# Gathered rows without columns of ones: the softmax weights copied into the weighed rows by ScalarE

## The chip, the core and the metric

The kernel runs on one core of a Trainium2 chip. The metric is the device time of one execution in microseconds (us). A core has a matrix engine (TensorE, PE in the profile; PEld is its weight load), a vector engine (VectorE, DVE), a scalar engine (ScalarE, ACT), GpSimd (POOL), which also issues the indirect DMAs, and SyncE (SP), which only issues DMAs and handles semaphores. Each engine runs its own instructions in order; between engines only semaphores order the work.

## The reference

Two graph layers over the same graph with 12500 nodes of 256 features (8 heads of 32) and 200000 edges that are sorted by their destination. Layer 0 is a transformer layer, layer 1 a graph attention layer. The part that the change touches is the softmax over the edges of a node, in both layers:

```
layer 0: score = sum(K[src] * Q[dst]) / sqrt(32) + edge_bias        (per head)
layer 1: score = leaky_relu(el[src] + er[dst], 0.2)                 (per head)
ex   = exp(score - segment_max(score, dst)[dst])
out  = segment_sum(ex / segment_sum(ex, dst)[dst] * value[src], dst)
```

`value` is V in layer 0 and `feat` in layer 1. The kernel divides last: it sums `ex * value` and `ex` itself per node and divides the one by the other.

## The kernel before

**Phases.** In order of time: a short start that works out which tile of 128 nodes each step serves; the projection of all nodes (98 tiles), which stores the tables `kv_tab` (K and V) and `q_tab`; the edge phase of layer 0; the dense phase between the layers (98 tiles: projection, norms, feed-forward part, and the table `ft_tab` of layer 1); the edge phase of layer 1; a final pass of 98 tiles.

**The edge phase.** It has 880 steps, in 110 blocks of 8 (`ST`). A step takes one span of 256 edges (two chunks of 128) and one tile of 128 nodes. There are 782 spans; where a span reaches into the next tile, it is used by a second step. POOL gathers the rows of a span with two indirect DMAs of 128 rows each (`gathers`, line 525) into a ring of 18 spans in layer 0 and 32 in layer 1. Before it reuses a place of the ring it waits until the last weighing of that place is done (`ev_made`, line 520).

**A step on the engines**, at these distances in steps (in `turn` of each engine's `edge_phase`):
- ACT makes the one-hot matrices of the edges' nodes (`distances`, `onehots`), some steps ahead.
- PE (`spread`) multiplies them with the queries (layer 0) or with `er` (layer 1), two steps ahead.
- DVE makes the scores: `product` and `reduce` in layer 0, `el_er` in layer 1 (with `members`, line 1227, which makes the transposed one-hots).
- Once per block, the maxima are found by scans on DVE with transposes on PE in between (`chunk_scans`, `row_scans`, `whole_scans`, `below_maximum`), and at s == 3 ACT makes the exponentials of the block before (`weights`, line 688, tile `ex`).
- 12 steps after the scores, DVE multiplies the gathered values with `ex` (`weigh`, line 1284, tile `ev`, which has places for 4 steps), and PE (`agg`) multiplies the one-hots with `ev` and so sums over the edges. Two steps later DVE adds the result to the running sums (`add`, line 1299); ACT stores four steps' sums at a time (`sum_store`).

**The columns of ones.** A value row is kept as 8 heads of 33 floats, of which the 33rd is 1.0. So `weigh` leaves `ex` itself in the 33rd column, and `agg` sums it with the values: this gives the denominator. The ones are written once into the four `kvo` buffers (line 1067) and into `fo` (line 1357), and then stored with every tile's rows in `kv_tab` (520 floats a row: 256 of K, 264 of V) and `ft_tab` (272 floats: 264 of `feat`, 8 of `el`). Every gather brings them back.

**Order of the queues.** SP starts the load of a step's queries or nodes (lines 375, 444) and tells DVE that a span has landed (`landed`, line 387), which POOL has signalled (line 532). At the head of each block DVE, SP and POOL load 8 or 16 registers from tables (`slots`, `spans_of`), which tell where each step's rows lie.

Of the kernel before, what the change touches and what calls it, by code (L numbers as in the profile page):

```python
# [26 lines left out]
P = 128  # L27
# [15 lines left out]
KVW = D + HV  # L43
FTW = HV + H
# [91 lines left out]
def build(nc, x, last, edges, span_src, Wq, Wk, Wv, Wp, bp, g1, b1n, g2, b2n, W1, b1, W2, b2,  # L136
          Wl, bl, Wg, al, ar, gb, out):
    ctx = ExitStack()
    with ctx:
# [150 lines left out]
        for name in """arep_made pat ats_made ohd oh_made oht_tr  # L290
            oht_cp oh0_made qexp prodd redd sadd smade s_tr scan_a rows_mm rows_cp row carried xy_cp cols_mm scan_b rx_made
            r_exp r_mm rm_made m_tr dmade ex_made ev_made agg accd resc init0 init1""".split():
            E_[name] = sem(name)
# [27 lines left out]
        def hv(ap):  # L321
            return ap.rearrange("p (h w) -> p h w", h=H)
# [257 lines left out]
        def _(act):  # L580
# [105 lines left out]
            def weights(B):  # L686
                act.wait_ge(E_["dmade"], B.c + 1)
                act.activation(ex[:, B.par, :], df[:, :], ACT.Exp).then_inc(E_["ex_made"], 1)  # L688

            def sum_store(layer, B, h):  # L690

                act.wait_ge(E_["accd"], B.c * ST + 4 * h + 4)
                r = (2 * B.n + h) * 4 * P
                act.dma_start(sums[r:r + 4 * P, :].rearrange("(p j) w -> p j w", j=4),
                              acc[:, B.par, 4 * h:4 * h + 4, :]).then_inc(acs[layer][B.par], 16)
# [7 lines left out]
            def edge_phase(layer):  # L703
                def turn(B):
                    A = B.on(-1)
                    for s in range(ST):
# [33 lines left out]
                        if s == 3 and A.live:  # L740
                            weights(A)

# [71 lines left out]
        def _(pe):  # L814
# [84 lines left out]
            def agg(B, s):  # L899
                pe.wait_ge(E_["ev_made"], B.c * ST + s + 1)  # L900
                o = sums_bank(B, s)
                mm(o, oh[:, B.tri, 2 * s, :], ev[:, s % 4, 0, :], True, False)
                mm(o, oh[:, B.tri, 2 * s + 1, :], ev[:, s % 4, 1, :], False, True).then_inc(E_["agg"], 1)
# [148 lines left out]
        def _(dve):  # L1052
# [13 lines left out]
            for kvo in kvos:  # L1066
                c0.did(V.memset(kvo[:, D:KVW], 1.0))
# [30 lines left out]
            def q_turn(t, slots, laps):  # L1098
# [15 lines left out]
                if not isinstance(t, int) or t >= 2:  # L1114
                    dve.wait_ge(S_["q_mm"], t - 1)
                    c = slots[2]
                    wait(dve, S_[f"q_st{c}"], 48 * laps[2])
                    V.tensor_copy(hv(kvos[c][:, D:KVW])[:, :, 0:HD],
                                  hv(bank[4 + c % 2][:, 0:D])).then_inc(S_["q_vq"], 1)
# [92 lines left out]
            def el_er(B, s, at):  # L1212
                dve.wait_ge(S_["rows_rdy"], B.c * ST + s + 1)
                dve.wait_ge(E_["qexp"], B.c * ST + s + 1)
                V.tensor_tensor(hc(sred[:, :])[:, :, 2 * s:2 * s + 2], step_rows(1, at)[:, :, HV:FTW].rearrange("p c h -> p h c"),  # L1215
                                bank[2 + s % 2][:, 0:2 * H].rearrange("p (c h) -> p h c", h=H),
                                ALU.add).then_inc(E_["sadd"], 1)
# [62 lines left out]
            def weigh(layer, B, s, at):  # L1280
                if s == 0:
                    dve.wait_ge(E_["ex_made"], B.c + 1)
                val = step_rows(0, at)[:, :, KVW - HV:KVW] if layer == 0 else step_rows(1, at)[:, :, 0:HV]
                V.tensor_tensor(ev[:, s % 4, :, :].rearrange("p k (h w) -> p k h w", h=H),  # L1284
                                val.rearrange("p k (h w) -> p k h w", h=H),
                                hc(ex[:, B.par, :])[:, :, 2 * s:2 * s + 2].rearrange("p h k -> p k h")
                                .unsqueeze(3).to_broadcast([P, 2, H, HD + 1]),
# [69 lines left out]
            c1.seq(V.memset(fo[:, 0:HV], 1.0))  # L1357
# [26 lines left out]
            def m_turn(t):  # L1384
# [20 lines left out]
                if on(4, t):  # L1405
                    dve.wait_ge(S_["m_mm2"], t - 3)
                    wait(dve, S_["m_sft"], 16 * (t - 4))
                    V.tensor_tensor(hv(fo[:, 0:HV])[:, :, 0:HD], hv(bank[7][:, 0:D]), hv(v_lge[:, 0:D]),
                                    ALU.add).then_inc(S_["m_fo"], 1)
                    V.tensor_tensor(fo[:, HV:FTW], bank[7][:, D:D + H], v_lge[:, D:D + H],  # L1410
# [96 lines left out]
```

## Time and profile before

| | |
|---|---|
| median of 3 runs | 6099.34 us (6095.61 to 6106.41) |
| the profiled execution | 6105.02 us, of which the span of the trace is 6103.1 us |
| busy share of the span | PE 89%, PEld 71%, DVE 81%, ACT 52%, POOL 61% |
| mean granted clock of TensorE | 0.902 of full speed |
| DMA | 1313.62 MB, mean 215 GB/s |
| edge phase, layer 0 | products from 377.8 to 2772.1 us |
| edge phase, layer 1 | gathers from 3767.8 to 5843.4 us |

A busy share is a mean over phases with different limits, so each phase is read by itself. A row of the windows view gives the busy time of each engine in a stretch and the number of its instructions; a row of the groups view gives the count of a kind of instruction, its total and mean time, and how long its engine had been idle before it and what ended that. Instructions of an engine overlap a little: the mean length of one is longer than the time from its start to the next one's start.

### The profile page before, as it was taken

The numbers are of one execution on the slowest core, as the hardware profiler recorded it, in microseconds if no ns is written. First come the engines' busy times: TensorE is split into PE (matmuls) and PEld (weight loads), VectorE is DVE, ScalarE is ACT, GpSimd is POOL, SyncE is SP. The second block draws the span as 40 slices with busy tenths as digits, with TensorE's granted clock in tenths as the row PEclk, the third lists the DMA queues.
The fourth block names the chain that finished last, engine by engine and source line by source line (L and its number), as shares of the span: only waits on it lengthen the run. The fifth ranks groups of instructions, "written<-read, shape, count | busy, mean of one in ns | idle before, by whom it ended". The sixth has DMA issues, their size and how long they took to land. (4 is left out here: it accounts for less than half of the span.)

```text
span 6103.1 us, 127510 instructions
## 1 busy us (share of the span) xinstructions
PE 5456.4 (89%) x26094; PEld 4304.6 (71%) x26094; DVE 4918.7 (81%) x12464; ACT 3153.0 (52%) x10275; POOL 3719.7 (61%) x4022
## 2 busy tenths in 40 slices
PE   8978888888888888887999998899999999999988
PEld 5556666666666666666999997677777777777766
DVE  4479999999999999996777775778778778777764
ACT  3455555555555555552333334555555556555533
POOL 1146666666666666662444445777777777777733
PEclk9999999999999999998999998777777777777789
DMA  5678888888888888883222223777777777777767
GB/s 177 211 225 282 275 271 274 271 271 273 272 273 270 271 273 273 272 269 108 85 84 84 84 84 110 213 222 218 217 219 221 219 219 222 216 217 219 221 194 230
DMA packets 723027, 1313.62 MB, mean 215 GB/s; under 512 B 109087, under 2 KB 502131, under 8 KB 722420
## 3 DMA queue, kind: packets, MB, share of 16 engines
q0 software_dynamic: 200192, 634.41, 37.2%
q1 hardware_dynamic: 444802, 422.18, 23.3%
q10 hardware_dynamic: 77426, 250.73, 10.6%
q14 instruction: 445, 3.65, 0.2%
q8 instruction: 162, 2.65, 0.2%
HBM read 964.16 MB, written 342.73 MB: 214 GB/s over the span
## 5 line engine op out<-in xcount | busy, mean ns | idle before, releaser
L816 PE MATMUL bank<-ev,oh 128*128 128x264 f32 x7040 | 2287.7, 455 | 90.7 <-DVE ev L1284 89.6
L525 POOL DMA_INDIRECT Gf<-kv_tab,srcs x1564 | 1541.1, 985 | 858.9 <-issue 465.4
L525 POOL DMA_INDIRECT Gf<-ft_tab,srcs x1564 | 1600.3, 1023 | 483.2 <-issue 420.1
L816 PEld LDWEIGHTS bank<-ev,oh 128*128 128x128 f32 x7040 | 1465.4, 221 | 346.8 <-DVE ev L1284 126.1
L816 PE MATMUL bank<-Gf 128*128 128x128 f32 (+3 forms) x6480 | 1261.7, 346 | 21.3 <-ACT Gf L805 14.4
L816 PE MATMUL bank<-qs,oht 128*128 128x256 f32 x3520 | 955.7, 394 | 319.9 <-DVE prod L1193 319.8
L1284 DVE TENSOR_TENSOR ev<-Gf,ex 128x528 f32<-128x528 f32 x1760 | 1236.8, 703 | 2.1 <-ACT ex L688 1.3
L816 PEld LDWEIGHTS bank<-Gf 128*128 128x128 f32 x6480 | 965.7, 191 | 220.2 <-issue 98.1
L621 ACT ACTIVATE absd<-lane,dlocs 128x128 f32<-128x128 f32 x3520 | 1112.8, 389 | 4.2 <-DVE bms L1166 3.7
L816 PEld LDWEIGHTS bank<-qs,oht 128*128 128x128 f32 x3520 | 599.6, 190 | 543.8 <-issue 370.9
L1299 DVE SCALAR_TENSOR_TENSOR acc<-acc,same,bank 128x264 f32<-128x264 f32 x1540 | 738.3, 479 | 28.3 <-PE bank L816 25.4
L1193 DVE TENSOR_TENSOR prod<-Gf,bank 128x512 f32<-128x512 f32 x880 | 600.5, 682 | 116.8 <-SPq L387 106.4
L502 POOL TENSOR_TENSOR vr<-vr,mhalf 128x1 f32<-128x1 f32 x392 | 248.5, 634 | 717.5 <-DVE vr L1373 418.8
L626 ACT ACTIVATE oh<-absd,ones 128x512 f32<-128x512 f32 x880 | 631.6, 718 | 10.9
L1199 DVE TENSOR_REDUCE sred<-prod 128x16 f32<-128x512 f32 x880 | 596.2, 678 | 0.3
L582 ACT ACTIVATE oht<-bank 128x512 f32<-128x512 f32 x440 | 261.2, 594 | 299.2 <-PE bank L819 293.7
L816 PEld LDWEIGHTS bank<-erq,prod 128*128 128x128 f32 x1760 | 352.5, 271 | 65.8 <-issue 34.8
L770 ACT ACTIVATE Gf<-bank,Gf 128x128 f32<-128x128 f32 x784 | 223.6, 369 | 289.4 <-PE bank L816 289.4
L816 PE MATMUL bank<-erq,prod 128*128 128x8 f32 x1760 | 345.1, 306 | 18.7 <-DVE sred L1215 18.0
L1215 DVE TENSOR_TENSOR sred<-Gf,bank 128x16 f32<-128x16 f32 x880 | 147.3, 167 | 246.9 <-PE bank L816 120.3
L652 ACT ACTIVATE rm<-bank,oh 128x8 f32<-128x8 f32 x220 | 78.6, 357 | 512.3 <-PE bank L816 506.3
L816 PEld LDWEIGHTS bank<-erq,oht 128*128 128x128 f32 x1760 | 274.5, 217 | 84.6 <-issue 53.5
(160 smaller groups left out, 6095.4 us busy)
## 6 DMA issues: line engine op xcount, KB each, us to landing
sums<-acc ACTq DMA_DIRECT2D x440, 528.0 KB
qs<-q_tab SPq DMA_DIRECT2D x880, 128.0 KB
qs<-dst_tab SPq DMA_DIRECT2D x880, 128.0 KB
Gf<-sums SPq DMA_DIRECT2D x196, 132.0 KB, 2.1
kv_tab<-Gf SPq DMA_DIRECT2D x98, 260.0 KB, 2.1
Gf<-in_x SPq DMA_DIRECT2D x196, 128.0 KB, 2.1
Gf<-kv_tab,srcs POOLq DMA_INDIRECT x1564
Gf<-ft_tab,srcs POOLq DMA_INDIRECT x1564
```

Source lines behind the costliest of these rows:

```text
L502: pool.tensor_tensor(vr[:, 2 * k + 1:2 * k + 2], vr[:, 2 * k:2 * k + 1], mhalf[:, :], ALU.pow).then_inc(done, 1)
L525: pool.indirect_dma_start(out=rows[layer][:, m % SLOTS[layer], k, :], out_offset=None, in_=tab, in_offset=bass.IndirectOffsetOnAxis(ap=src ...
L582: act.activation(o, i_, ACT.Copy).then_inc(s, 1)
L621: act.activation(absd[:, g % 2, k, :], lane[:, :], ACT.Abs, scale=-1.0, bias=dloc[:, B.n, 4 * g + k:4 * g + k + 1]).then_inc(E_["ohd"], 1)
L626: act.activation(oh[:, B.tri, 4 * g:4 * g + 4, :].rearrange("p c n -> p (c n)"), absd[:, g % 2, :, :].rearrange("p c n -> p (c n)"), ACT.R ...
L770: act.activation(gT[:, f * P:(f + 1) * P], bank[2 + f // 4][:, (f % 4) * P:(f % 4 + 1) * P], ACT.Gelu, bias=v_b1[:, f:f + 1]).then_inc(S_[ ...
L816: return nc.tensor.matmul(o, a, r, start=first, stop=end)
L1193: V.tensor_tensor(prod[:, s % 2, :, :], step_rows(0, at)[:, :, 0:D], bank[2 + s % 2][:, :].rearrange("p (k n) -> p k n", k=2), ALU.mult).t ...
L1199: V.tensor_reduce(hc(sred[:, :])[:, :, 2 * s:2 * s + 2].rearrange("p h c -> p c h"), prod[:, s % 2, :, :].rearrange("p k (h w) -> p k h w" ...
L1215: V.tensor_tensor(hc(sred[:, :])[:, :, 2 * s:2 * s + 2], step_rows(1, at)[:, :, HV:FTW].rearrange("p c h -> p h c"), bank[2 + s % 2][:, 0: ...
L1284: V.tensor_tensor(ev[:, s % 4, :, :].rearrange("p k (h w) -> p k h w", h=H), val.rearrange("p k (h w) -> p k h w", h=H), hc(ex[:, B.par, : ...
L1299: V.scalar_tensor_tensor(acc[:, B.par, s, :], prev, same[:, B.n * ST + s:B.n * ST + s + 1], sums_bank(B, s), ALU.mult, ALU.add).then_inc(E ...
```

## The change

The 33rd columns leave the tables. `kv_tab` has 512 floats a row, `ft_tab` 264. `weigh` multiplies 32 floats a head instead of 33 and leaves the 33rd column of `ev` alone. A new function on ACT, `weights_column`, copies the 16 values of `ex` (2 chunks of 8 heads) of a step into the 33rd columns, one step ahead of PE's `agg` in the order of the queues (`step_at(B, s - 11)` against `s - 12`). Before it writes, ACT waits until `agg` of four steps earlier has read that place of `ev`. `agg` waits for the new semaphore `exs_made` in addition to `ev_made`. The writing of ones (lines 1067 and 1357) is gone.

```
-KVW = D + HV
-FTW = HV + H
+KVW = 2 * D
+FTW = D + H
...
+            def weights_column(B, s):
+
+                if s == 0:
+                    act.wait_ge(E_["ex_made"], B.c + 1)
+                p, r = step_at(B, s - 4)
+                if p.live:
+                    act.wait_ge(E_["agg"], p.c * ST + r + 1)
+                copy(ev[:, s % 4, :, :].rearrange("p k (h w) -> p k h w", h=H)[:, :, :, HD],
+                     hc(ex[:, B.par, :])[:, :, 2 * s:2 * s + 2].rearrange("p h k -> p k h"), E_["exs_made"])
...
                         if s == 3 and A.live:
                             weights(A)
+                        C, r = step_at(B, s - 11)
+                        if C.live:
+                            weights_column(C, r)
...
             def agg(B, s):
+                pe.wait_ge(E_["exs_made"], B.c * ST + s + 1)
                 pe.wait_ge(E_["ev_made"], B.c * ST + s + 1)
...
-            for kvo in kvos:
-                c0.did(V.memset(kvo[:, D:KVW], 1.0))
...
-                    V.tensor_copy(hv(kvos[c][:, D:KVW])[:, :, 0:HD],
-                                  hv(bank[4 + c % 2][:, 0:D])).then_inc(S_["q_vq"], 1)
+                    V.tensor_copy(kvos[c][:, D:KVW], bank[4 + c % 2][:, 0:D]).then_inc(S_["q_vq"], 1)
...
-                V.tensor_tensor(hc(sred[:, :])[:, :, 2 * s:2 * s + 2], step_rows(1, at)[:, :, HV:FTW].rearrange("p c h -> p h c"),
+                V.tensor_tensor(hc(sred[:, :])[:, :, 2 * s:2 * s + 2], step_rows(1, at)[:, :, D:FTW].rearrange("p c h -> p h c"),
...
-                val = step_rows(0, at)[:, :, KVW - HV:KVW] if layer == 0 else step_rows(1, at)[:, :, 0:HV]
-                V.tensor_tensor(ev[:, s % 4, :, :].rearrange("p k (h w) -> p k h w", h=H),
+                val = step_rows(0, at)[:, :, D:KVW] if layer == 0 else step_rows(1, at)[:, :, 0:D]
+                V.tensor_tensor(ev[:, s % 4, :, :].rearrange("p k (h w) -> p k h w", h=H)[:, :, :, 0:HD],
                                 val.rearrange("p k (h w) -> p k h w", h=H),
                                 hc(ex[:, B.par, :])[:, :, 2 * s:2 * s + 2].rearrange("p h k -> p k h")
-                                .unsqueeze(3).to_broadcast([P, 2, H, HD + 1]),
+                                .unsqueeze(3).to_broadcast([P, 2, H, HD]),
                                 ALU.mult).then_inc(E_["ev_made"], 1)
...
-            c1.seq(V.memset(fo[:, 0:HV], 1.0))
...
-                    V.tensor_tensor(hv(fo[:, 0:HV])[:, :, 0:HD], hv(bank[7][:, 0:D]), hv(v_lge[:, 0:D]),
-                                    ALU.add).then_inc(S_["m_fo"], 1)
-                    V.tensor_tensor(fo[:, HV:FTW], bank[7][:, D:D + H], v_lge[:, D:D + H],
+                    V.tensor_tensor(fo[:, 0:D], bank[7][:, 0:D], v_lge[:, 0:D], ALU.add).then_inc(S_["m_fo"], 1)
+                    V.tensor_tensor(fo[:, D:FTW], bank[7][:, D:D + H], v_lge[:, D:D + H],
```

## Rows read from the trace of the kernel before

**Rows 1.** Windows: from:to, length, busy us (count) per engine, PE clock, DMA share, GB/s

```profile
100.00:200.00 100.00, 96.60 (x321) 53.64 (x322) 49.17 (x161) 41.49 (x130) 17.52 (x32) 1.00 0.63 211
...
600.00:2500.00 1900.00, 1618.35 (x7827) 1246.08 (x7826) 1813.01 (x3651) 1095.57 (x3217) 1212.23 (x1237) 1.00 0.87 272
3000.00:3600.00 600.00, 600.00 (x3936) 551.50 (x3935) 430.27 (x1397) 210.39 (x697) 291.32 (x444) 1.00 0.27 85
4000.00:5800.00 1800.00, 1675.44 (x7038) 1326.07 (x7037) 1433.56 (x4089) 1059.58 (x3895) 1387.08 (x1356) 0.74 0.78 219
```

**Rows 2.** Groups by form, 600 to 2500 us (layer 0): busy us, mean ns | idle before, releasers

```profile
L525 POOL DMA_INDIRECT Gf<-kv_tab,srcs x1237 | 1213.1, 981 | 687.8 <-issue 350.7 <-DVE ev L1284 274.4 <-DMA Gf<-kv_tab,srcs 62.7
...
L1284 DVE TENSOR_TENSOR ev<-Gf,ex 128x528 f32<-128x528 f32 x696 | 490.4, 705 | 0.0
L1193 DVE TENSOR_TENSOR prod<-Gf,bank 128x512 f32<-128x512 f32 x695 | 474.2, 682 | 80.6 <-SPq L387 74.9 <-issue 5.7
...
L1299 DVE SCALAR_TENSOR_TENSOR acc<-acc,same,bank 128x264 f32<-128x264 f32 x608 | 292.4, 481 | 0.3 <-PE bank L816 0.3
...
L1269 DVE TENSOR_TENSOR df<-S,bank 128x128 f32<-128x128 f32 x86 | 24.1, 281 | 0.0
```

**Rows 3.** Timeline of DVE at the head of a block of layer 0

```profile
1615.99 0.28 DVE L1208 TENSOR_TENSOR S<-sred,bms 128x128 f32<-128x128 f32 x1
1617.16 0.69 DVE L1193 TENSOR_TENSOR prod<-Gf,bank 128x512 f32<-128x512 f32 x1 [0.89 <-SPq L387]
```

**Rows 4.** Waits of SP's queue, 600 to 2500 us: total us, times, longest

```profile
SPq L375 <- PE bank L816: 717.2, 442, 2.5
SPq L387 <- POOLq L532: 1.1, 2, 0.7
```

**Rows 5.** Groups by form, 0 to 30 us (the start)

```profile
L1082 DVE TENSOR_TENSOR same<-tile_of 128x879 f32<-128x879 f32 x1 | 1.1, 1074 | 0.0
```

**Rows 6.** Groups by form, 4000 to 5800 us (layer 1)

```profile
L525 POOL DMA_INDIRECT Gf<-ft_tab,srcs x1356 | 1387.9, 1024 | 413.2 <-issue 357.5 <-DMA Gf<-ft_tab,srcs 35.3 <-DVE ev L1284 20.4
...
L582 ACT ACTIVATE erq<-er_all 128x8 f32 x760 | 151.3, 199 | 91.5 <-issue 74.4 <-PE bank L816 16.6
```

**Rows 7.** Line 525, the gathers of layer 1: shortest/median/longest ns, first and last start

```profile
L525 POOL DMA_INDIRECT Gf<-ft_tab,srcs x1564: 942/947/1753, 3767.8 to 5843.4; - x196
```

**Rows 8.** Timeline in layer 1: start us, length us, idle before it

```profile
5820.65 0.70 DVE L1284 TENSOR_TENSOR ev<-Gf,ex 128x528 f32<-128x528 f32 x1
5820.71 1.45 POOL L525 DMA_INDIRECT Gf<-ft_tab,srcs  x1 [0.30 <-issue]
...
5822.47 0.95 POOL L525 DMA_INDIRECT Gf<-ft_tab,srcs  x1 [0.30 <-issue]
```

**Rows 9.** Timeline in layer 1: ACT and PE around a step's weighed sum

```profile
4610.56 0.28 ACT L663 ACTIVATE ats<-bank 128x128 f32<-128x128 f32 x1 [3.13 <-PE bank L819]
...
4611.10 1.26 ACT L621 ACTIVATE absd<-lane,dlocs 128x128 f32<-128x128 f32 x4
...
4612.27 0.20 ACT L582 ACTIVATE erq<-er_all 128x8 f32 x1
...
4612.89 0.91 PE L816 MATMUL bank<-ev,oh 128*128 128x264 f32 x3
```

**Rows 10.** Timeline at the start and at the head of the dense phase

```profile
3.02 1.12 DVE L1067 MEMSET Gf<- 128x264 f32 x4
4.06 0.11 DVE L1068 TENSOR_SCALAR last_t<-last_i 128x7 int32<-128x7 int32 x1
...
10.22 3.27 PE L816 MATMUL bank<-oh,ones 128*128 128x440 f32 x4 [10.22 <-DVE ev L1074]
...
2816.09 0.28 DVE L1357 MEMSET Gf<- 128x264 f32 x1 [22.48 <-DMA Gf<-in_L_gnn_b_lin]
2816.45 0.17 DVE L1389 TENSOR_SCALAR Gf<-Gf 128x8 f32<-128x8 f32 x1
```

**Rows 11.** DMA queue of the gathers, 1000 to 1500 us: packets, MB, share of 16 engines

```profile
q0 software_dynamic: 26055, 86.73, 59.5%
```

More of the change, by code:

```diff
@@ L291, in build @@
             oht_cp oh0_made qexp prodd redd sadd smade s_tr scan_a rows_mm rows_cp row carried xy_cp cols_mm scan_b rx_made
-            r_exp r_mm rm_made m_tr dmade ex_made ev_made agg accd resc init0 init1""".split():
+            r_exp r_mm rm_made m_tr dmade ex_made exs_made ev_made agg accd resc init0 init1""".split():
             E_[name] = sem(name)
```

## Prediction

> **What bounds the kernel now.** I read the windows first, because the limit changes with the phase [rows 1]. In the first stretch (projection) PE is busy for 96.6 of 100 us, in the dense phase for 600 of 600: these two are PE's, and the change takes no matrix work away. In layer 0's edge phase DVE is busy for 1813 of 1900 us and PE for only 1618. In layer 1's, DVE has 20% left and PE 7%, and POOL is busy for 1387 of 1800 us, which looks loose and is not.
>
> In layer 0 the groups tell where DVE's missing 87 us are [rows 2]: 80.6 of them stand ahead of the product, 0.3 ahead of the sum, none ahead of the weighing. The 1900 us hold 695 products, which is 87 blocks, and 87 times 0.89 us [rows 3] is 77 us: one gap at each block's head. SP's signal is named as its releaser. But SP waits for landed rows only 2 times in this stretch, and 442 times for PE [rows 4], so the rows are there early; DVE's own 16 register loads at a block's head are the simpler cause. POOL is ahead too: 274 us of its idle time are waits for a free place in the ring. So layer 0 goes at the rate at which DVE gets through its list, 1900/695 = 2.73 us a step.
>
> In layer 1 POOL's group [rows 6] adds up to the window: 1387.9 us busy and 413.2 idle, and the idle time is 0.305 us ahead of each of 1356 DMAs. That is no waiting: 0.30 also stands before DMAs that waited for nothing [rows 8]. POOL issues without a break, at 1.024 + 0.305 = 1.329 us each. All 1564 take 2078 us, and the gathers last from 3767.8 to 5843.4 [rows 7]. Layer 1 goes at POOL's issue rate.
>
> **Weigh, in layer 0.** It loses 16 of 528 elements. Two DVE products of two tensors of other lengths give the price of an element: 879 take 1074 ns [rows 5], 128 take 281 ns [rows 2], so (1074 - 281)/751 = 1.056 ns, and 16 cost 16.9 ns. The product with 512 elements, 682 ns against 705, agrees within 6 ns, though it reads PSUM. Nothing else on DVE changes in a step, and DVE hardly waits, so 880 x 16.9 ns = **14.9 us** fall out. Bounds: 0 (the output now leaves gaps, and a gapped write could cost what it saves) and 880 x 23 ns = 20 us.
>
> **Weigh, in layer 1.** DVE has room here, so directly its saving is worth nothing. But half of the gathers take 947 ns or less, and the mean is 1024 [rows 7, 6]. A case shows why [rows 8]: the DMA at 5820.71, issued while a weighing was running, took 1.45 us, the next one 0.95. Its extra 0.50 us end at 5821.21, when the weighing (from 5820.65) has streamed its 528 elements, 528 x 1.056 = 0.56 us. So a gather that is issued into a weighing waits for the end of its streaming. As a check: steps are 1800/761 = 2.365 us, the chance to hit one is 0.56/2.365 = 24%, the mean wait 0.28 us, together 66 ns for a DMA, of 77 measured. With 512 elements each such wait ends 16.9 ns earlier: 1564 x 0.24 x 16.9 ns = **6.3 us**, on the path. Bounds: 0, if the phases shift so that hits become more frequent, and 1564 x 16.9 = 26 us, if every gather waited; I take the middle price because it explains the mean.
>
> The Trainium skill (SBUF — State Buffer, section "Who interferes with whom") says that a VectorE operation with two SBUF inputs contends with GpSimd instructions that read SBUF, but infers that such an operation does not hold up the generation of descriptors. By the first half the 6.3 us stand, by the second they would be 0 and the time 6.3 us longer. The case above speaks for the first.
>
> **The column copies on ACT.** The nearest row is a copy of 128x8 from SBUF in 199 ns [rows 6]; 16 elements need hardly more, and four distances of 128x128 take 1.26 us together [rows 9], 0.32 us each, so neighbours overlap. I take 0.2 us: 1760 x 0.2 = 352 us of ACT time. It lies beside other work: ACT is busy for 58% and 59% of the edge phases [rows 1] and would go to 65% and 67%. What matters is whether a column is later than the weighed rows that PE needs anyway. The tightest place I found is in layer 1 after the link sums [rows 9]: ACT comes out of a 3.13 us wait at 4610.56, has its four distances done at 4612.36 and the copy of `er` at 4612.47; the column would be ready at about 4612.7, and PE took up the weighed sum at 4612.89. It fits by 0.2 us. ACT's other operations behind the column move back by 0.2 us each step and are caught up in ACT's next wait for PE, which is 3.13 us here. The added wait for `agg` of four steps earlier is long fulfilled in ACT's order. PE's added wait instruction has no row; from 0 to some 50 ns a step it stays inside PE's slack (layer 1: 1675.44/761 = 2.20 us busy of 2.365, so 0.16 us). Cost 0; if this cover is gone it costs as in the third rival.
>
> **Start and head of the dense phase.** The four memsets delay the next DVE instruction from 3.02 to 4.06 us, and PE's first product waits for that chain [rows 10]: **1.0 us** (at least 0, if something behind hides it). The memset at 2816.09 delays its successor by 0.36 us at a point where all wait for DVE: **0.4 us**.
>
> **Bytes.** Gathered rows are 1.5% (layer 0) and 3% (layer 1) shorter; the gathers take 59.5% of the DMA engines' time [rows 11] and nobody waits for them. Stores of the tables in the two PE-bound phases shrink likewise. 0 us.
>
> **Sum.** 14.9 + 6.3 + 1.0 + 0.4 = 22.6 us. The profiled execution took 6105.0 us (1.9 beyond its span), which gives 6082.4. It stands 5.7 us above the median of 6099.3, so against the median the forecast is **6076.7 us**, -0.37%. A measurement of this kernel can tell about 0.2%, 12 us, from no change.
>
> **Rivals.**
> 1. *The block's head takes layer 0's saving back.* If the gap [rows 3] is a wait for SP at a pace that does not depend on DVE, a shorter weighing only lengthens it. For it: SP is named. Against it: SP's own waits. Only 7.7 us remain: 6091.6. Chance 0.12.
> 2. *The weighing gets no shorter*, since its output now has gaps. Against it: the elements are single floats in either case. 1.4 us remain, 6097.9. Chance 0.07.
> 3. *Slower: the columns come late in layer 1.* ACT reaches the column only behind its long groups, PE then idles before the weighed sum. It decides from a mean lateness of 0.16 us a step, where PE's busy 2.20 us plus waiting pass POOL's 2.365. At 0.3 us a step the phase grows by 880 x 0.14 = 120 us, less the 16 us of layer 0 and the start: 6203. For it: a margin of only 0.2 us at one step in eight. Against it: ACT idles about 3 us twice a block. Chance 0.06.
> 4. *Slower: the gathers of layer 0 slow down.* Rows of exactly 2048 bytes start at equal places modulo 2048. DMA engines are busy for 0.87 [rows 1], so if the gathers' 59.5% took 22% longer they would be full; at 40% longer the phase grows by 0.87 + 0.24 = 1.11, 11% of 2394 us, to 6350. No row speaks for it. The Trainium skill (DMA: Bandwidth & Descriptors, "Latency and other measured facts") reports loss at row pitches of large powers of two, from 512 KiB up, which is far from here. Chance 0.02.
> 5. *More than forecast*: layer 1's gathers are hit much less, as they fall elsewhere between the weighings, up to 26 us there: 6057. Chance 0.06.
>
> The forecast itself has the remaining 0.67, with its own range 6069 to 6086. Taking in rival 1 and the nearer half of rival 5, the range is 6067 to 6094. Faster by over 0.2% (below 6087.1): the forecast and rival 5, less a little for noise, 0.69. Within: rivals 1 and 2 and that noise, 0.22. Slower: rivals 3 and 4 and what I have not seen, 0.09.
>
> **What would show it.** Right: weighings of 128x512 at 686 to 688 ns, DVE's gap at a block's head still 0.89 us, layer 0's products taking 2379 us from first to last instead of 2394; in layer 1 POOL's mean at 1020 ns and its last gather about 2069 us after its first; new ACT copies near 0.2 us, with no idle time of PE ahead of the weighed sum that ends on ACT. Wrong: a gap at the block's head that grows by 0.14 us (rival 1), weighings at 703 ns (rival 2), PE idle in front of `agg` with ACT's copy as its releaser (rival 3), POOL's mean unchanged or higher.

## The result, and the profile after

| | before | after |
|---|---|---|
| median (5 runs each) | 6099.43 us (6095.61 to 6106.41) | 6133.27 us (6126.67 to 6146.65) |
| ratio, 95% interval | | 1.0051 (1.004 to 1.0063) |
| the profiled execution, its span | 6105.02, 6103.1 us | 6129.33, 6127.4 us |
| layer 0, first product to last weighing | 2413.3 us | 2398.3 us |
| between, to the first gather of layer 1 | 976.6 us | 977.6 us |
| layer 1, first gather to last sum | 2107.9 us | 2146.6 us |
| start, last pass | 377.8, 227.4 us | 377.7, 227.2 us |

The forecast was 6076.7 us, faster; the kernel became slower by 0.5%. Layer 0 gave what was forecast, layer 1 took 38.7 us more.

Windows of the changed kernel (columns as in [rows 1]):

```profile
600.00:2500.00 1900.00, 1625.68 (x7876) 1250.67 (x7874) 1812.34 (x3671) 1174.73 (x3937) 1215.61 (x1246) 1.00 0.84 271
4000.00:5800.00 1800.00, 1643.72 (x6879) 1303.56 (x6879) 1387.08 (x3997) 1122.88 (x4557) 1390.43 (x1345) 0.74 0.75 213
```

In layer 0 DVE does more in the same time at the same busy share. In layer 1 every engine but ScalarE does less (PE 6879 instructions instead of 7038), and only ScalarE, which has the copies, is clearly busier (POOL by 3 us): PE idles for 156 us of the 1800 instead of 125. DVE's groups in layer 0, 600 to 2500 us:

```profile
L1295 DVE TENSOR_TENSOR ev<-Gf,ex 128x512 f32<-128x512 f32 x700 | 480.7, 687 | 0.0
L1204 DVE TENSOR_TENSOR prod<-Gf,bank 128x512 f32<-128x512 f32 x699 | 476.1, 681 | 80.5 <-SPq L387 74.1 <-issue 6.3
```

687 ns a weighing against 705, and the idle time at the blocks' heads unchanged (80.5 against 80.6 us) [rows 2]. The groups of layer 1, 4000 to 5800 us, PE's first, then its weight load, ScalarE's copies, POOL's gathers:

```profile
L829 PE MATMUL bank<-ev,oh 128*128 128x264 f32 x2973 | 1146.7, 522 | 110.4 <-DVE ev L1295 56.8 <-ACT ev L582 52.1 <-issue 0.2
...
L829 PEld LDWEIGHTS bank<-ev,oh 128*128 128x128 f32 x2974 | 675.1, 251 | 229.6 <-ACT ev L582 70.0 <-issue 62.8
...
L582 ACT ACTIVATE ev<-ex 128x16 f32<-128x16 f32 x744 | 162.4, 218 | 3.1
...
L525 POOL DMA_INDIRECT Gf<-ft_tab,srcs x1345 | 1391.4, 1035 | 409.9 <-issue 352.9 <-DMA Gf<-ft_tab,srcs 34.4 <-DVE ev L1295 22.6
```

The same group of the kernel before has 72.5 us of idle time of PE ahead of the weighed sum, 71.7 of them ended by DVE:

```profile
L816 PE MATMUL bank<-ev,oh 128*128 128x264 f32 x3044 | 1182.2, 525 | 72.5 <-DVE ev L1284 71.7 <-issue 0.2
```

Now it is 110.4, and a new releaser, ScalarE's copy, stands beside DVE. This is what the forecast had named as the sign of its third rival. One place of it (timeline of the changed kernel, start, length, idle time before):

```profile
4560.51 1.26 ACT L621 ACTIVATE absd<-lane,dlocs 128x128 f32<-128x128 f32 x4
...
4561.68 0.19 ACT L582 ACTIVATE erq<-er_all 128x8 f32 x1
4561.78 0.21 ACT L582 ACTIVATE ev<-ex 128x16 f32<-128x16 f32 x1
4561.90 0.70 ACT L626 ACTIVATE oh<-absd,ones 128x512 f32<-128x512 f32 x1
4562.04 0.74 PEld L829 LDWEIGHTS bank<-ev,oh 128*128 128x128 f32 x4 [0.52 <-ACT ev L582]
4562.05 0.94 PE L829 MATMUL bank<-ev,oh 128*128 128x264 f32 x3 [0.43 <-ACT ev L582]
```

It is the fourth step of a block, the very place of [rows 9]: the column follows the four distances and `er`, ends at 4561.99, and PE has been idle for 0.43 us. But the sums per step of a block, worked out from the records of PE over the 110 blocks, show that this is only a part. Mean idle time of PE ahead of the weighed sum in layer 1, steps 0 to 7, and the shortest distance from the end of a weighing to the start of its sum:

```
step      0     1     2     3     4     5     6     7    shortest distance
before   0.01  0.01  0.01  0.00  0.05  0.15  0.19  0.37   0.05 us
after    0.01  0.05  0.00  0.27  0.05  0.17  0.19  0.45   0.15 us
```

Steps 3 and 1 have late columns. At step 7 no column is late (it ends 1.1 us ahead at least), and yet PE waits longer, and no sum starts less than 0.15 us behind its weighing, where it was 0.05. So there were two suspects.

That PE, and no longer POOL, sets the pace can be read at the end of the layer. Before, PE's last weighed sum ends 31.8 us after the last gather starts; in the changed kernel it ends 57.9 us after it. POOL still issues without a break (1391.4 + 409.9 us fill the window), and PE falls behind it, as the ring of 32 spans allows. The last gather itself starts 2088.2 us after the first, 12.6 us later than before; the part on why the prediction was wrong comes back to this.

### The profile page after: what moved, and what is told of

Its sections match the earlier page's. It is cut to its first block and busy times, and to the rows that moved or that the text cites. A ratio compares the mean times of both kernels' runs of the same rounds, so it can differ in the third digit from the quotient of the medians.

```text
span 6127.4 us, 131243 instructions
## 1 busy us (share of the span) xinstructions
PE 5453.4 (89%) x26094; PEld 4304.3 (70%) x26094; DVE 4886.3 (80%) x12459; ACT 3347.9 (55%) x12035; POOL 3722.2 (61%) x4022
## 5 line engine op out<-in xcount | busy, mean ns | idle before, releaser
L525 POOL DMA_INDIRECT Gf<-ft_tab,srcs x1564 | 1612.9, 1031 | 483.2 <-issue 416.4
L1295 DVE TENSOR_TENSOR ev<-Gf,ex 128x512 f32<-128x512 f32 x1760 | 1205.0, 685 | 2.5 <-ACT ex L688 1.6
L582 ACT ACTIVATE ev<-ex 128x16 f32<-128x16 f32 x1760 | 385.2, 219 | 16.7 <-DVE acc L1310 5.0
```

Of the source, the lines that this page charges most:

```text
L525: pool.indirect_dma_start(out=rows[layer][:, m % SLOTS[layer], k, :], out_offset=None, in_=tab, in_offset=bass.IndirectOffsetOnAxis(ap=src ...
L582: act.activation(o, i_, ACT.Copy).then_inc(s, 1)
```

## The experiments

The theories, by the letters that the expectations use: **L**, late columns; **W**, the second wait of the weighed sum costs 0.10 us by itself; **A**, ScalarE's load alone; **C**, nothing of layer 1 but the clock or heat that layer 0 leaves. Later W is split: **W1**, any second wait costs it; **W2**, only if the wait that PE really waits for stands in the separate instruction. **P** is the prediction's claim on gathers: one that is issued into a weighing waits for the end of its streaming. Kernels under one heading ran on one chip beside the kernel before (under "Where the wait has its price" two chips); ratios are to it, with 95% intervals.

### First four: a chip of 7316 us, on which small waits do not show

Layer 0 changed alone (tables and weighing of layer 1 as before, its sum with one wait):

```
-FTW = D + H
+FTW = HV + H
...
-                        if C.live:
+                        if C.live and layer == 0:
...
-                pe.wait_ge(E_["exs_made"], B.c * ST + s + 1)
+                if B.layer == 0:
+                    pe.wait_ge(E_["exs_made"], B.c * ST + s + 1)
                 pe.wait_ge(E_["ev_made"], B.c * ST + s + 1)
...
```

> The change in layer 0 only; layer 1 keeps its columns of ones, its 528-element weighing and its single wait. If the loss is all in layer 1 (every theory below), layer 0 keeps its 15 us and layer 1 its 2108 us: 6084 to 6086 us, ratio 0.9975. If shorter weighings in layer 0 shift something that layer 1 or the dense phase gives back, it stays near 6099.

The kernel before with one wait more:

```
             def agg(B, s):
+                pe.wait_ge(E_["ex_made"], B.c + 1)
                 pe.wait_ge(E_["ev_made"], B.c * ST + s + 1)
```

> The kernel before, but the weighed sum on TensorE waits for a second semaphore (ex_made), which has long been reached; nothing else changes. Theory W (a second wait in front of the weighed sum costs 0.10 us wherever the sum would start as soon as the weighing ends): in layer 1 the shortest distance from the end of a weighing to the sum rises from 0.05 to 0.15 us, at three or four steps of a block, so 0.3 to 0.4 us a block and 15 to 40 us in all: 6115 to 6140. Theory L (late columns alone cost the time): a second wait is free, 6099.

The kernel before with the copies, into a tile that nobody reads (ScalarE waits for its own earlier copies instead of for PE's sums):

```
...
+                wait(act, E_["exs_made"], B.c * ST + s - 3)
+                copy(spare[:, :, :].rearrange("p k (h w) -> p k h w", h=H)[:, :, :, HD - s % 4],
+                     hc(ex[:, B.par, :])[:, :, 2 * s:2 * s + 2].rearrange("p h k -> p k h"), E_["exs_made"])
...
```

> The kernel before, with ScalarE's 1760 small copies at the same places, into a spare tile that nobody reads and nobody waits for (the copies wait for ScalarE's own earlier copies instead of for TensorE's sums). If ScalarE's added load is what costs (its other results reach TensorE later): layer 1 loses 20 us or more, 6120. Theories L and W both say that the load is covered: 6095 to 6105.

The changed kernel with the columns one step earlier:

```
                         if s == 3 and A.live:
                             weights(A)
-                        C, r = step_at(B, s - 11)
-                        if C.live:
+                            weights_column(A, 0)
+                        C, r = step_at(B, s - 10)
+                        if C.live and r:
                             weights_column(C, r)
```

> The changed kernel with every column one step earlier in ScalarE's order (step 0's right behind the exponentials, then step s - 10 instead of s - 11). The sum still has two waits. Theory L: no sum finds its column missing, 0.3 us a block is back in layer 1, about 35 us: 6095 to 6100. Theory W: half of the loss stays, 0.10 us wherever the sum meets the end of a weighing: 6105 to 6120.

Measured: this chip ran the kernel before in 7316.19 us, 20% above the 6099 of all I had reasoned from. Ratios 1.0059 (1.0036 to 1.0082), 1.0006 (0.9989 to 1.0022), 0.9998 (0.9983 to 1.0014), 0.9996 (0.9981 to 1.0011). The window of layer 1 in the run with the second wait shows the other regime:

```profile
5000.00:6800.00 1800.00, 1473.20 (x5372) 1146.67 (x5373) 1106.63 (x3118) 813.11 (x2981) 1067.52 (x1032) 0.65 0.62 167
```

No engine is near full, PE neither: 1800 us hold 1032 gathers instead of 1356, and the clock is 0.65. A tenth of a microsecond lost or won at PE's sum does not show in the end there. The distances can still be read: shortest 0.05 us with one wait (first and third), 0.15 us with two (second and fourth).

The first run missed its expectation of 0.9975: it was slower than the kernel before. Its layer 0 took 2988 us, the other three 2924 to 2934. Its trace shows late columns at work in layer 0. PE's groups there, 1000 to 2500 us, first of this run, then of the run with the early columns:

```profile
L829 PE MATMUL bank<-ev,oh 128*128 128x264 f32 x1784 | 522.3, 419 | 193.2 <-ACT ev L582 187.9 <-issue 5.4
```

```profile
L830 PE MATMUL bank<-ev,oh 128*128 128x264 f32 x1816 | 511.9, 407 | 0.6 <-ACT ev L582 0.4
```

On this chip ScalarE is stopped for up to 10 us at a time ahead of `ats` (last section), and at step 3 of a block the column stands behind that stop: PE waits 3.2 us there on average in layer 0, half of the sums starting 0.05 us behind their column. On the chips of 6100 us no column of layer 0 ends less than 0.41 us ahead of its sum. How much of the 54 to 64 us this makes up is not shown, since with early columns PE waits for ScalarE elsewhere (115 us for the one-hots in the same window).

### The same questions on a chip of 6105 us

> The changed kernel itself, beside the kernel before on this chip. If this chip runs the kernel before in about 6100 us: ratio 1.005, first gather of layer 1 to last sum 2147 us, and every theory agrees, it is the control for the others. If it runs it in about 7300 us, as the chip of the last four runs did (there the whole of the change's parts moved the time by 0.06% or less): theory L (late columns) and theory W (the second wait) expect a ratio of 1.000 to 1.002 there, since PE is behind in layer 1 all the time and its idle time ahead of the weighed sum is small either way; theory A (ScalarE's load alone) expects 1.000.

> The changed kernel with each column copied one step earlier in ScalarE's order (and the first of a block straight after the exponentials). On a chip of 6100 us: theory L (the columns of the fourth and second step of a block come late) expects PE's idle time ahead of the fourth step's weighed sum to fall from 0.27 us to under 0.05, layer 1 to take 2110 to 2125 us instead of 2147, and the ratio to the kernel before to be 0.998 to 1.001. Theory W (the second semaphore wait itself costs 0.10 us of each weighed sum that PE waits for) expects only a third of it back: ratio 1.003 to 1.004. Theory A (ScalarE's load) expects 1.005 as before, since the copies are all still there.

> The kernel before with one more wait instruction ahead of PE's weighed sum, on a semaphore that was reached long ago. On a chip of 6100 us: theory W expects the shortest distance from the weighing's end to the sum's start to go from 0.05 to 0.15 us and the time up by 880 x 0.1 x the share of steps at which PE waits (about a third) = 15 to 30 us in layer 1 and none in layer 0: ratio 1.002 to 1.005. Theory L and theory A expect 1.000.

> The change in layer 0 alone; layer 1 keeps its column of ones, its weighing of 528 elements and its single wait. On a chip of 6100 us: products of layer 0 in 2379 to 2381 us instead of 2394, layer 1 at 2108 us, ratio 0.9975 (6084 us). If the time is not below that of the kernel before, the loss of 39 us in layer 1 does not come from anything that layer 1 does differently (theory C: it is the phase of the clock or of the heat that layer 0 leaves behind).

Measured, beside 6105.11 us: the changed kernel 1.0064 (1.0047 to 1.008), columns early 1.0026 (1.0017 to 1.0035), second wait alone 1.006 (1.0045 to 1.0074), layer 0 alone 0.9971 (0.9962 to 0.998).

Layer 0 alone settles C: its trace has layer 1 at 2098.6 us and no loss. The early columns take PE's idle time at step 3 from 0.24 to 0.00 us and give back 0.4%; late columns cost time, but not the whole of it: 1.0026 lies between what L (0.998 to 1.001) and W (1.003 to 1.004) expected, and layer 1 took 2139.5 us, not L's 2110 to 2125. And one wait instruction, on a semaphore reached long ago, costs by itself as much as the whole change. W has the direction and the distance (0.14 us) right; its price of 1.006 lies above the 1.002 to 1.005 that was expected. PE's group in layer 1 with that wait:

```profile
L816 PE MATMUL bank<-ev,oh 128*128 128x264 f32 x2978 | 1184.3, 536 | 92.8 <-DVE ev L1285 91.0 <-ACT ex L688 1.0 <-issue 0.3
```

How can a fulfilled wait cost anything? By line, the trace shows an instruction that the kernel before does not have (its columns: shortest, median, longest ns, first and last start), in this run and in the changed kernel:

```profile
L901 PEldq EVENT_SEMAPHORE  x1760: 51/51/51, 405.2 to 5917.6; - x196
```

```profile
L914 PEldq EVENT_SEMAPHORE  x1760: 51/51/51, 404.3 to 5898.5; - x196
```

Both lines, 901 here and 914 there, are the wait for the weighing (`ev_made`), which is written last. The wait written first is carried by the weight load itself, whose operands in the trace name that semaphore. So PE learns that the weighing is done in an instruction of its own, and only then takes up the load. At a step where it waits, the separate instruction starts 0.04 us behind the weighing and takes 0.05, and the sum starts 0.06 us behind its end; together that is the 0.15. In the timeline of this run:

```profile
4596.18 0.70 DVE L1285 TENSOR_TENSOR ev<-Gf,ex 128x528 f32<-128x528 f32 x1
...
4596.99 0.50 PEld L816 LDWEIGHTS bank<-ev,oh 128*128 128x128 f32 x2 [0.50 <-ACT ex L688]
4597.02 0.78 PE L816 MATMUL bank<-ev,oh 128*128 128x264 f32 x1 [0.43 <-DVE ev L1285]
```

The weighing ends at 4596.88, the sum starts 0.14 us later. The releaser "ACT ex" of the load is the inference from the wait that it carries; the real one is DVE. The same holds for a part of the "ACT ev" above.

The Trainium skill (Perfetto Trace Analysis, section "Identifying Dependency Chains") notes that an instruction that waits on several engines may have EventSemaphore instructions inserted ahead of it. The 1760 of line 914 agree; which wait goes where, and its price, the runs here show.

### Which of the two waits stands alone

The next runs turn the order round. First the kernel before with the second wait:

```
             def agg(B, s):
                 pe.wait_ge(E_["ev_made"], B.c * ST + s + 1)
+                pe.wait_ge(E_["ex_made"], B.c + 1)
```

> The kernel before with the same added wait as in the run that gave 1.006, but written behind the wait for the weighing instead of ahead of it. The trace of that run shows how two waits are carried: the weight load of the weighed sum carries the wait that is written first (there the exponentials, long there), and the one written last (the weighing) stands in a semaphore instruction of its own, 51 ns long, whose end is 0.08 us ahead of the load. Theory W2 (what costs is that the wait that is really waited for stands in the separate instruction) expects that now the separate instruction is over long before and the load itself waits for the weighing: shortest distance from the weighing's end to the sum's start 0.05 us, ratio 0.999 to 1.001 on a chip of 6100 us. Theory W1 (any second wait costs 0.10 us there) expects 0.15 us and 1.005 to 1.007 again.

The changed kernel, with `ev_made` first and `exs_made` second:

> The changed kernel with the two waits of the weighed sum written the other way round, columns as late as before. Theory W2: where PE waits for the weighing the distance is 0.05 us again; at the fourth step of a block it waits for the column through the separate instruction and the late column costs what it did. The parts so far, relative to the kernel before: layer 0 -0.0029, second wait +0.0060, late columns +0.0038. So ratio 1.000 to 1.002. Theory W1: 1.005 to 1.007 as the changed kernel.

The same with the early columns:

> The changed kernel with the columns copied one step earlier and the two waits of the weighed sum written the other way round. Theory W2 with theory L: both costs of layer 1 are gone and layer 0's saving is left, ratio 0.996 to 0.998 (6080 to 6093 us), layer 1 at 2098 to 2110 us from first gather to last sum, mean granted clock back at 0.900 or above. Theory W1: 1.002 to 1.003 as with early columns alone. Theory A (ScalarE's load or the copies' writes cost by themselves): above 0.999 too.

And the copies alone once more:

> The kernel before with ScalarE's 1760 copies added, into a tile that nobody reads, and nothing else. Theories L and W2: 0.999 to 1.001, since no engine waits for them; ScalarE's busy share goes from 59% to 65% of layer 1. Theory A (the copies themselves cost, by ScalarE's lateness with one-hots and transposes): 1.002 or more.

Measured, beside 6099.67 us: 1.0002 (0.9993 to 1.0011), 1.0063 (1.0049 to 1.0077), 0.9976 (0.9966 to 0.9985), 1.001 (1.0001 to 1.0019).

The first is as clean as it gets: the same two waits in the other order, and 0.6% are gone. The separate instructions are still there, but line 901 of this kernel is the wait for the exponentials:

```profile
L901 PEldq EVENT_SEMAPHORE  x1760: 51/51/51, 404.3 to 5866.1; - x196
```

In its timeline the sum starts 0.05 us behind the weighing (4577.36 + 0.70 to 4578.11):

```profile
4577.36 0.70 DVE L1285 TENSOR_TENSOR ev<-Gf,ex 128x528 f32<-128x528 f32 x1
...
4578.11 0.50 PEld L816 LDWEIGHTS bank<-ev,oh 128*128 128x128 f32 x2 [0.49 <-DVE ev L1285]
```

The second missed: with late columns the swap brings nothing (1.0063, not 1.000 to 1.002), and by its ratio alone W1 (1.005 to 1.007) would have been right. The prices do not add up. Its idle time at step 7 is down to 0.34 us, but at step 3 it is up to 0.32, since there the late wait is the one that now stands alone: its shortest distance from column to sum is 0.14 us instead of 0.05. And either cost alone is enough to make PE's chain the longest of layer 1. The third, with both costs away, beats the kernel before, by 0.24%. The copies themselves cost 0.1%, at most 0.2%, below the 1.002 that A asked for; theory A is not the cause.

### Where the wait has its price

```
             def agg(B, s):
+                if s >= 4:
+                    pe.wait_ge(E_["ex_made"], B.c + 1)
                 pe.wait_ge(E_["ev_made"], B.c * ST + s + 1)
```

and the same with `s < 4`, and the kernel before with half a weighing in layer 1, whose result therefore leaves out the second 128 rows of each step:

```
-                V.tensor_tensor(ev[:, s % 4, :, :].rearrange("p k (h w) -> p k h w", h=H),
-                                val.rearrange("p k (h w) -> p k h w", h=H),
+                kk = 2 if layer == 0 else 1
+                V.tensor_tensor(ev[:, s % 4, 0:kk, :].rearrange("p k (h w) -> p k h w", h=H),
+                                val[:, 0:kk, :].rearrange("p k (h w) -> p k h w", h=H),
...
```

> The kernel before with the extra wait (written ahead of the wait for the weighing) at the steps 4 to 7 of each block only: there PE idles ahead of the weighed sum, 0.05, 0.15, 0.19 and 0.37 us on average in layer 1. Theory W2: nearly all of the second wait's cost, ratio 1.004 to 1.007. A rival, that the extra semaphore instruction costs time in PE's queue wherever it stands (880 of 1760 here), expects half of 1.006: 1.003.

> The same at the steps 0 to 3 only, where the weighing is over long before (idle time ahead 0.01 us each). Theory W2: ratio 1.000 to 1.001. The rival with a cost wherever it stands: 1.003.

> The kernel before; in layer 1 the weighing multiplies only the first 128 of a step's 256 gathered rows (264 elements a lane instead of 528), so layer 1's result leaves out the rest. Theory P (a gather that is issued into a weighing waits for the end of its streaming, 66 ns of the mean 1024): half the chance of a hit and half the wait, so 16 ns instead of 66, mean of a gather 0.97 us and layer 1 at (0.97 + 0.305) x 1564 = 1995 to 2010 us unless PE stops it earlier. The rival (the extra time of a gather comes from something else that happens to run beside the weighing): mean 1.015 to 1.025 as in all kernels so far, and layer 1 at 2090 to 2108 us.

This chip ran the kernel before in 7322.84 us, and again the waits did not show: 0.9998 (0.9985 to 1.0012) and 0.9991 (0.9975 to 1.0008). But a gather's own length can be read there as well. The gathers of layer 1 with the whole weighing (the first of these runs; 1548 of them fall in the stretch read), then with half of it:

```profile
L525 POOL DMA_INDIRECT Gf<-ft_tab,srcs x1548 | 1590.0, 1027 | 1116.2 <-DVE ev L1286 625.0 <-issue 491.2
```

```profile
L525 POOL DMA_INDIRECT Gf<-ft_tab,srcs x1564 | 1516.6, 970 | 1208.9 <-DVE ev L1285 738.1 <-issue 469.8 <-DMA Gf<-ft_tab,srcs 0.9
```

970 ns, as theory P had it (0.97 us), against 1027. The longest of its gathers took 1432 ns, against 1574 in the first of these runs. The whole ratio is 0.9984 (0.9967 to 1.0001), and layer 1 was not shortened to the 1995 to 2010 us that P expected; here POOL waits 738 us for places in the ring, so nothing of it could reach the end.

The two waits once more, and a version in which DVE instead of PE waits for the column (with the early columns):

```
             def agg(B, s):
-                pe.wait_ge(E_["exs_made"], B.c * ST + s + 1)
                 pe.wait_ge(E_["ev_made"], B.c * ST + s + 1)
...
-                if s == 0:
-                    dve.wait_ge(E_["ex_made"], B.c + 1)
+                dve.wait_ge(E_["exs_made"], B.c * ST + s + 1)
```

> The same kernel as in the first run of the last call (that chip ran the kernel before in 7323 us, where no wait of PE shows in the time). On a chip of 6100 us: theory W2 1.004 to 1.007 (PE idles ahead of the weighed sum at these steps), a cost of the semaphore instruction wherever it stands 1.003.

> The extra wait at the steps 0 to 3 only, where the weighing is over long before. On a chip of 6100 us: theory W2 1.000 to 1.001, a cost wherever it stands 1.003.

> The changed kernel with early columns and DVE, not PE, waiting for the column ahead of each weighing, so that the weighed sum keeps its single wait for the weighing. On a chip of 6100 us: layer 1 at 2100 to 2110 us as with the swapped waits; in layer 0 a wait more on DVE, which bounds it. If it costs DVE nothing (the wait is carried by the weighing itself): ratio 0.996 to 0.998; if DVE's second instruction costs some 0.05 us a step at 880 steps: 44 us, 1.003 to 1.006.

Measured, beside 6104.09 us: 1.007 (1.0056 to 1.0083), 1.0 (0.9991 to 1.0009), 0.9973 (0.9962 to 0.9985). The price sits wholly at the steps 4 to 7, where PE arrives before the weighing is done; at the steps 0 to 3 the same instruction is free. PE's group in layer 1 of the two, steps 4 to 7 first:

```profile
L816 PE MATMUL bank<-ev,oh 128*128 128x264 f32 x2994 | 1182.4, 533 | 93.6 <-DVE ev L1286 91.2 <-ACT ex L688 1.5
```

```profile
L816 PE MATMUL bank<-ev,oh 128*128 128x264 f32 x3032 | 1191.9, 531 | 72.9 <-DVE ev L1286 72.5 <-issue 0.2
```

A cost of the instruction wherever it stands, expected at 1.003 for both, is ruled out. And the wait given to DVE costs nothing visible: its layer 0 takes 2397.9 us, as the others with the change.

### What the wait sets going

All runs on chips of about 6100 us, layer 1 (us). Idle and busy are PE's, per block, from its records over 90 blocks; "sum" is the idle time ahead of the weighed sums; "low" is the time per block in which the granted clock was at its lower level (1.2 GHz, half):

```
                             layer 1   block   sum   all idle   busy    low
before                       2107.9    18.92   0.76    1.31    17.61    9.93
layer 0 alone                2098.6    18.85   0.76    1.18    17.67   10.16
copies alone                 2106.0    18.92   0.75    1.19    17.73   10.31
second wait, swapped         2103.1    18.93   0.77    1.26    17.67   10.09
wait at steps 0 to 3         2115.9    19.00   0.77    1.20    17.80   10.43
columns early, swapped       2106.7    18.98   0.71    1.27    17.71   10.16
columns early, DVE waits     2110.3    18.97   0.70    1.10    17.87   10.58
wait at steps 4 to 7         2139.3    19.26   1.00    1.39    17.87   10.84
columns early                2139.5    19.23   0.95    1.33    17.90   10.96
second wait                  2152.6    19.34   1.00    1.36    17.98   11.12
after, waits swapped         2162.6    19.49   1.00    1.58    17.91   10.51
after                        2146.6    19.38   1.19    1.68    17.70   10.24
after, again                 2174.0    19.57   1.16    1.65    17.92   10.77
```

Two groups: with 0.70 to 0.77 us of idle time ahead of the sums a block takes 18.85 to 19.00 us, with 0.95 or more it takes 19.23 to 19.57. The same two groups stand apart at the end of the layer: PE's last sum ends 29.9 to 40.5 us after the last gather's start in the first group, and 70.5 to 73.3 us after it in the second (57.9 in the first trace of the changed kernel). In the second group PE's chain is the longest.

The second wait adds 0.24 us of idle time ahead of the sums (0.76 to 1.00), but the block grows by 0.49 (18.85 to 19.34, on the same chip). Of this, 0.31 us are matmul time: busy 17.98 instead of 17.67, with the clock 0.96 us longer at its lower level. A matmul of the weighed sum takes 386 ns at the upper and 647 ns at the lower level, so by estimate 0.96 us more at the lower one add 0.96 x (1 - 386/647) = 0.39 us to the same work. But this is one pair of single executions. On another chip the wait at steps 4 to 7 adds 0.23 us of idle time ahead of the sums against the wait at steps 0 to 3, and the block grows by only 0.26, of which 0.07 are matmul time. And in the changed kernel beside the kernel before, 0.37 of the block's 0.46 us are idle time, and the lower level has 53% of the block in both. So nearly all of its loss there is waiting; in the repeated run beside layer 0 alone it is 0.47 of 0.72 us. Whether waiting also brings the clock down is not shown.

## Why the prediction was wrong, point by point

- **Weigh in layer 0**, forecast 14.9 us: layer 0 is 15.0 us shorter, each weighing 687 instead of 705 ns. Right, and rivals 1 and 2 fell.
- **Start**, forecast 1.0 us: PE's first product starts at 9.14 instead of 10.22 us [rows 10], but the first product of layer 0 only 0.1 us earlier. The lower bound was the truth: something behind hides it. **Head of the dense phase**, 0.4 us: the stretch takes 975.1 to 978.8 us in all these traces, so it can't be seen.
- **Bytes**: 0 us, and rival 4 fell; layer 0's DMA share went from 0.87 to 0.84.
- **Weigh in layer 1**, forecast 6.3 us by POOL's waits for the weighing. The mechanism is real: before, the 406 gathers that were issued while a weighing ran took 1156 ns on average, the other 1158 took 976; and the mean is 970 ns with half a weighing. Its size could not be read from one trace, since the number of such hits moves with every kernel. In the changed one 477 gathers were hit, the mean went up from 1023 to 1031 ns over all 1564, and the last gather started 2088.2 us after the first, instead of 2075.6 (forecast: about 2069). That is the case that the prediction had put at its lower bound of 0, and it went past it. In the early and swapped version a gather takes 1020 ns, which is the forecast's figure by luck: the unchanged layer shows 1015 to 1026 ns. The one half of the Trainium skill's section (SBUF — State Buffer, "Who interferes with whom"), that a two-input VectorE operation contends with a GpSimd instruction that reads SBUF, agrees with this. Whether its inference that descriptor generation is not held up fails here is not shown: a gather also reads its row numbers (`srcs`) in SBUF, and no trace tells the two apart.
- **The failed step**: "PE's added wait instruction has no row; from 0 to some 50 ns a step it stays inside PE's slack (layer 1: 1675.44/761 = 2.20 us busy of 2.365, so 0.16 us). Cost 0". Both halves were wrong. The 0.16 us were no slack: of 1.31 us idle a block, 0.76 stood ahead of weighed sums, where PE waited for DVE, and what is added to such a wait lengthens the chain in full (0.23 us more there, 0.26 more a block, in the pair above). And the added instruction took 0.10 us exactly there, since it took over the wait that really waits. Its own length was not the error, and a row for it did exist; the trace of the kernel before has such instructions on PE's queue (count, shortest, median, longest ns):

```profile
L133 PEldq EVENT_SEMAPHORE  x2448: 51/51/582, 43.9 to 6093.4; - x189
```

The error was to take it as covered wherever it stands. POOL needs 1564 x 1.329/110 = 18.90 us a block, and an idle time of 0.24 us more at PE already brought 19.26 to 19.34: PE's chain must have been nearly as long as POOL's before. Busy shares of 93% and 77% hid that.
- **The columns**: "It fits by 0.2 us". That was one block. At step 3 the mean margin to PE was gone (70% of that step's sums in the repeated run start within 0.3 us of their column's end), worth 0.24 to 0.27 us a block. ScalarE's idle time did not serve as cover, as the forecast had it: in the window of the changed kernel it stands ahead of work for which ScalarE waits for PE, and only 3.1 us of it ahead of the columns:

```profile
L652 ACT ACTIVATE rm<-bank,oh 128x8 f32<-128x8 f32 x93 | 33.3, 358 | 202.9 <-PE bank L829 202.9
L582 ACT ACTIVATE wlf<-bank 1x384 f32<-1x384 f32 x93 | 44.8, 482 | 133.7 <-PE bank L832 133.5 <-issue 0.2
```

When it comes out of such a wait, the four distances (1.26 us) go first and the column after them. Rival 3 was this mechanism, with 0.06; its threshold of 0.16 us a step was the same slack. The real lateness, some 0.03 us a step (0.27/8), did its damage below it. The sign to watch for was named rightly, the threshold was not.

Of the loss of 38.7 us in layer 1, either part would have cost most alone (second wait 1.006; late columns with swapped waits 1.0063, though there the column's wait stands in the separate instruction, so that a late column costs 0.1 us more). Without both, layer 0's gain remains: **columns early and waits swapped, 6085.37 us (0.9976)**; with DVE waiting 6089.4 us (0.9973); the change in layer 0 alone 6088.33 us (0.9971). These three can't be told apart, and all beat both kernels.

## What to carry to other kernels

Busy time over the period of a step is no slack of an engine: look at what its idle time stands before, and if it is the loop of waits with another engine, every added 0.1 us lands in the sum. Where an instruction needs two semaphores, write the wait that really comes last in the place where the instruction itself carries it (here: first), and check in the trace that the separate semaphore instruction has the line of the other. A new producer for an old consumer should be given a distance of a whole step in its queue, not the last place in which it still fits in one looked-at block.

## What was not expected of the hardware

- A separate semaphore instruction on PE's queue takes 51 ns, and a sum that waited through it starts 0.14 to 0.15 us behind its releaser instead of 0.05. In layer 1's 880 steps this cost 0.6% of the kernel, in layer 0's nothing.
- These chips differ by 20%. Of those of the experiments, three ran the kernel before in 6099.67 to 6105.11 us, two in 7316.19 and 7322.84 us. On those, in the run with the second wait, PE's mean granted clock was 0.91 already in layer 0, and ScalarE and DVE had waits of up to 10 us that are put down to no instruction of this core ("remote"; total us, times, longest):

```profile
ACT ats L663 <- remote: 234.9, 34, 10.2
ACT oht L582 <- remote: 199.9, 46, 10.0
...
DVE prod L1194 <- remote: 110.3, 36, 4.9
```

What holds the core up there is open. Small changes can't be judged on such a chip: the second wait, 0.6% on the others, is 1.0006 (0.9989 to 1.0022) there, and layer 0 changed alone, a gain of 0.3% on the other, loses 0.6%.
